# Weights loaded in the order of their first use, late ones prepared behind the first convolution, and x loaded already turned

## The reference

```python
xz = x @ W_in                                  # (16, 512, 128) @ (128, 512)
x_in, z = jnp.split(xz, 2, axis=-1)
xp = jnp.pad(x_in, ((0, 0), (3, 0), (0, 0)))
xc = conv_general_dilated(xp, dw_kernel[:, None, :], ...)   # 4 taps, depthwise
xc = silu(xc @ pw_kernel + conv_bias)          # then x_dbl = xc @ W_x, delta, the scan over 8 states,
...                                            # y * silu(z) @ W_out
```

## Time and profile before

| | |
|---|---|
| median of 3 runs | 2472.59 us (2466.28 to 2479.43) |
| the profiled execution | 2474.75 us, its span 2472.9 us |
| PE busy | 2107.4 us, 85% of the span |
| DVE busy | 1962.8 us, 79% |
| ACT busy | 1427.6 us, 58% |
| POOL busy | 808.0 us, 33% |
| mean granted TensorE clock | 0.951 |

### The profile page before, as it was taken

The page is one execution under the profiler, slowest core; times in us unless marked ns, Lnnn a source line. Parts: engine busy times, 40 slices in busy tenths (PEclk is TensorE's granted clock), DMA queues, the critical chain, the costliest instruction groups (busy, mean ns, idle before and its releaser), DMA issues. The chain is left out here.

```text
span 2472.9 us, 52605 instructions
## 1 busy us (share of the span) xinstructions
PE 2107.4 (85%) x15800; PEld 1560.8 (63%) x15929; DVE 1962.8 (79%) x3681; ACT 1427.6 (58%) x3256; POOL 808.0 (33%) x1060
## 2 busy tenths in 40 slices
PE   4389898989989898989898989899889849999980
PEld 1147565656657565657575656566566749999980
DVE  2787989798988888888988897989885447777768
ACT  2366766666667675666767666666655413333334
POOL 0111424141415141423324241414141333333337
PEclk9699999999999999999999999999989969999995
DMA  3452424152433324243424241524230042122117
GB/s 118 103 126 61 107 69 117 50 124 61 111 86 81 102 64 102 65 114 78 108 69 101 68 116 51 124 60 111 72 92 14 30 151 59 55 60 59 55 52 196
DMA packets 160526, 212.88 MB, mean 86 GB/s; under 512 B 20296, under 2 KB 97104, under 8 KB 160064
## 3 DMA queue, kind: packets, MB, share of 16 engines
q1 hardware_dynamic: 138192, 144.20, 19.7%
q0 software_dynamic: 22272, 67.92, 13.4%
HBM read 134.71 MB, written 28.08 MB: 66 GB/s over the span
## 5 line engine op out<-in xcount | busy, mean ns | idle before, releaser
L1432 DVE TENSOR_TENSOR_SCAN hs<-decay,push 128x512 f32<-128x512 f32 x256 | 320.1, 1272 | 7.1
L1184 ACT ACTIVATE S<-banks,fall_tok 128x128 f32<-128x128 f32 x1024 | 278.8, 385 | 27.7 <-PE banks L816 27.4
L1003 PE MATMUL banks<-rowsT,w_here 128*128 128x128 f32 x2176 | 269.6, 278 | 6.5 <-DVE w_here L1774 6.5
L1003 PEld LDWEIGHTS banks<-rowsT,w_here 128*128 128x128 f32 x2176 | 256.0, 193 | 10.1 <-issue 9.1
L1853 POOL DMA_DIRECT2D y<-ch x96 | 88.1, 918 | 477.2 <-DVE ch L1440 374.5
L1944 POOL TENSOR_TENSOR qd<-q,q_fall 128x512 f32<-128x512 f32 x96 | 159.4, 1660 | 208.7 <-ACT chunk_fall L1169 208.7
L1540 DVE TENSOR_TENSOR S<-banks,S 128x512 f32<-128x512 f32 x256 | 167.8, 683 | 64.2 <-PE banks L828 44.9
L1985 POOL DMA_INDIRECT results_scratch<-rows_out,result_to x136 | 132.2, 972 | 241.2 <-ACT rows_out L1310 234.5
L1425 DVE TENSOR_TENSOR push<-du,b_all 128x1024 f32<-128x1024 f32 x128 | 198.1, 1547 | 2.0 <-DMA b_all<-bc_scratch 2.0
L1299 ACT ACTIVATE tanh_h<-banks 128x512 f32<-128x512 f32 x136 | 81.3, 598 | 203.3 <-PE banks L1003 203.3
L1547 DVE SCALAR_TENSOR_TENSOR oT<-tog,banks 128x512 f32<-128x512 f32 x128 | 87.2, 681 | 136.0 <-ACT sq L1152 135.9
(11 more groups left out here) (221 smaller groups left out, 5096.5 us busy)
## 6 DMA issues: line engine op xcount, KB each, us to landing
y<-ch POOLq DMA_DIRECT2D x96, 512.0 KB, 5.5
b_all<-bc_scratch SPq DMA_DIRECT2D x128, 256.0 KB, 3.9
c_all<-bc_scratch SPq DMA_DIRECT2D x128, 256.0 KB, 3.6
q_fall<-fall_scratch SPq DMA_DIRECT2D x192, 128.0 KB, 3.3
rows_in<-rows_scratch SPq DMA_DIRECT2D x136, 66.0 KB
both<-results_scratch SPq DMA_DIRECT2D x32, 256.0 KB, 3.4
w<-w_dram SPq DMA_DIRECT2D x3, 2048.0 KB, 9.6
x_tok<-x_dram SPq DMA_DIRECT2D x16, 256.0 KB, 3.2
```

The source lines that it names most:

```text
L1003: mm = pe.matmul(bank_h[:, u % 2, n, here], w_here[:, u % 2, n, here], x, start=True, stop=True)
L1184: ins = nc.scalar.activation(S[:, g, here], bank[:, here], ACT.Exp, bias=fall_tok[:, head:head + 1])
L1432: nc.vector.tensor_tensor_scan(hs[:, h, :], decay[:, n % 2, h, :], push[:, h, :], 0.0, ALU.mult, ALU.add).then_inc(s_scan, 1)
```

## The change

- The loads are split in three, each on its own semaphore and in this order on SP: `conv_loads` (`w_inT`, `taps`, `pw`), then x of sequence 0, then `front_loads` (`b_conv`, `w_x`, `w_dt`, `b_dt`, `a_log`, `w_z`, `d_skip`), then the other 23.
- PE's fold waits for the first group alone; ACT waits for the second before it starts, since it begins with the exponential of `a_log`; PE waits for the second before the first sequence.
- `w_tap` has two places and the fold uses banks 0 and 1 in turn.
- DVE's preparation of `w_out`, `w_k`, `w_o`, `w_sign` and the token numbers goes into `prepare_late`, after its part of the first convolution in stage 2 of round 0. PE waits for it, and PE and ACT for the remaining loads, at the start of round 1, POOL for the loads before its first round.
- The host also gives x with features first (`xT`); SP loads it straight into the 512 columns of `xT`. `x_tok`, PE's four transposes, ACT's copy and the ring's use `xT` go away; 97 uses are left. The next load now waits until z of the sequence before has been multiplied (stage 6), in place of the turn (stage 0).

```diff
-FRONT = {"xT": 0, "u0": 1, "u1": 2, "xdbl": 3, "dt0": 4, "dt1": 4, "z0": 6, "z1": 6}
+FRONT = {"u0": 1, "u1": 2, "xdbl": 3, "dt0": 4, "dt1": 4, "z0": 6, "z1": 6}
...
-        w_tap = S[:, 1, 2 * P:4 * P].rearrange("p (c n) -> p c n", c=HALVES)
+        w_tap = S[:, 3, :].rearrange("p (s c n) -> p s c n", s=2, c=HALVES)
...
+        conv_loads = [(w_inT[:], a["w_inT"]), (taps[:], a["taps"]), (pw[:], a["pw"])]
+        front_loads = [
+            (b_conv[:], a["b_conv"]), (w_x[:], a["w_x"]), (w_dt[DT_ROW:DT_ROW + 8, :], a["w_dt"]), (b_dt[:], a["b_dt"]),
+            (a_log[:], a["a_log"]), (w_z[:], a["w_z"]), (d_skip[:], a["d_skip"]),
+        ]
...
-        PREPARED = 12 + PAIRS
+        PREPARED, PREPARED_LATE = 9, 3 + PAIRS
...
         @block.sync
         def _(sp):
+            for dst, src in conv_loads:
+                sp.dma_start(dst, src).then_inc(s_w_first, 16)
+            sp.dma_start(xT[:, TAPS - 1:TAPS - 1 + T], a["xT"][0]).then_inc(s_x_loaded, 16)
+            for dst, src in front_loads:
+                sp.dma_start(dst, src).then_inc(s_w_front, 16)
             for dst, src in loads:
                 sp.dma_start(dst, src).then_inc(s_weights, 16)
...
                     if not first(n):
-                        sp.wait_ge(ring.full_sem("xT"), ring.full_at("xT", n - 1))
-                    sp.dma_start(x_tok[:], x_dram[bass.ds(n, 1)].rearrange("b p c d -> (b p) c d")
-                                 ).then_inc(s_x_loaded, 16)
+                        sp.wait_ge(ring.full_sem("z1"), ring.full_at("z1", n - 1))
+                        sp.dma_start(xT[:, TAPS - 1:TAPS - 1 + T], a["xT"][bass.ds(n, 1)].rearrange("b d t -> (b d) t")
+                                     ).then_inc(s_x_loaded, 16)
...
         def _(pe):
-            pe.wait_ge(s_weights, WEIGHTS)
+            pe.wait_ge(s_w_first, 16 * len(conv_loads))
             for t in range(TAPS):
                 pe.wait_ge(s_wtap, HALVES * (t + 1))
-                if t >= 1:
-                    pe.wait_ge(s_wconv, t)
+                if t >= 2:
+                    pe.wait_ge(s_wconv, t - 1)
                 for c in range(HALVES):
-                    mm = pe.matmul(ring_banks[:, 0, 0:2 * P], w_tap[:, c, :], pw[:, c, :],
+                    mm = pe.matmul(ring_banks[:, t % 2, 0:2 * P], w_tap[:, t % 2, c, :], pw[:, c, :],
                                    start=(c == 0), stop=(c == 1))
                 mm.then_inc(s_wmul, 1)
             pe.wait_ge(s_wconv, TAPS)
             pe.wait_ge(s_prep, PREPARED)
+            pe.wait_ge(s_w_front, 16 * len(front_loads))
...
-            def turn_input(n):
+            def convolve(h, n):
                 pe.wait_ge(s_x_loaded, at(n, 16, 16))
-                turn("xT", x_tok, n)
-
-            def convolve(h, n):
-                bank, full = fill(ring, f"u{h}", n, "xT")
+                bank, full = fill(ring, f"u{h}", n)
...
             def body(i, j, n):
+                if i is not None and first(i):
+                    pe.wait_ge(s_weights, WEIGHTS)
+                    pe.wait_ge(s_prep_late, PREPARED_LATE)
...
         def _(act):
-            act.wait_ge(s_weights, WEIGHTS)
+            act.wait_ge(s_w_front, 16 * len(front_loads))
             nc.scalar.activation(a_neg[:], a_log[:], ACT.Exp).then_inc(s_alog, 1)
...
-            def turn_input(n):
-                nc.scalar.copy(xT[:, TAPS - 1:TAPS - 1 + T], full(ring, "xT", n)).then_inc(ring.free_sem("xT"), 1)
...
         def _(dve):
-            dve.wait_ge(s_weights, WEIGHTS)
+            dve.wait_ge(s_w_first, 16 * len(conv_loads))
             for t in range(TAPS):
-                if t >= 1:
-                    dve.wait_ge(s_wmul, t)
+                if t >= 2:
+                    dve.wait_ge(s_wmul, t - 1)
...
+            dve.wait_ge(s_w_front, 16 * len(front_loads))
+            nc.vector.tensor_scalar(b_conv[:], b_conv[:], 0.5, None, ALU.mult).then_inc(s_prep, 1)
             dve.wait_ge(s_alog, 1)
             nc.vector.tensor_scalar(a_neg[:], a_neg[:], -1.0, None, ALU.mult).then_inc(s_prep, 1)
             dve.wait_ge(s_prep, PREPARED)
+            def prepare_late():
+                dve.wait_ge(s_weights, WEIGHTS)
+                for w in (w_out, w_k):
+                    nc.vector.tensor_scalar(w[:], w[:], 0.5, None, ALU.mult).then_inc(s_prep_late, 1)
...
+                dve.wait_ge(s_prep_late, PREPARED_LATE)
...
+                    if h == FRONT["u1"] and first(n):
+                        prepare_late()
...
         def _(pool):
...
             pool.wait_ge(s_prep, PREPARED)
+            pool.wait_ge(s_weights, WEIGHTS)
```

More of the change, by code:

```diff
@@ L418, in build @@
         bank_y, bank_rows = banks[:, 4:6, :], banks[:, 6:8, :]
+        s_w_first = sem("conv_weights_loaded")
+        s_w_front = sem("front_weights_loaded")
         s_weights = sem("weights_loaded")
+        s_prep_late = sem("late_weights_prepared")
         s_wtap = sem("w_tap_ready")
@@ L1046, in _ @@
                 act.wait_ge(s_wmul, t + 1)
-                nc.scalar.activation(w_conv[:, t, :], ring_banks[:, 0, 0:2 * P], ACT.Copy, scale=0.5
+                nc.scalar.activation(w_conv[:, t, :], ring_banks[:, t % 2, 0:2 * P], ACT.Copy, scale=0.5
                                      ).then_inc(s_wconv, 1)
+            act.wait_ge(s_prep, PREPARED)
             def full(ring, use, it):
@@ L1256, in body @@
             def body(i, j, n):
+                if i is not None and first(i):
+                    act.wait_ge(s_weights, WEIGHTS)
                 if j is not None:
@@ L1356, in _ @@
             nc.vector.memset(state[:], 0.0).then_inc(s_prep, 1)
-            dve.wait_ge(s_weights, WEIGHTS)
+            dve.wait_ge(s_w_first, 16 * len(conv_loads))
             for t in range(TAPS):
-                if t >= 1:
-                    dve.wait_ge(s_wmul, t)
+                if t >= 2:
+                    dve.wait_ge(s_wmul, t - 1)
                 for c in range(HALVES):
-                    nc.vector.tensor_scalar(w_tap[:, c, :], w_inT[:, c, :], taps[:, c, t:t + 1], None,
+                    nc.vector.tensor_scalar(w_tap[:, t % 2, c, :], w_inT[:, c, :], taps[:, c, t:t + 1], None,
                                             ALU.mult).then_inc(s_wtap, 1)
-            for w in (b_conv, w_out, w_k):
-                nc.vector.tensor_scalar(w[:], w[:], 0.5, None, ALU.mult).then_inc(s_prep, 1)
-            for t in range(PAIRS):
-                nc.vector.tensor_scalar(w_o[:, t, :], w_o[:, t, :], norm_w[:, t:t + 1], 0.5 * HID ** 0.5, ALU.mult, ALU.mult
-                                        ).then_inc(s_prep, 1)
-            nc.vector.tensor_scalar(w_less, w_ffn[:], 0.0, None, ALU.is_lt).then_inc(s_sign, 1)
-            nc.vector.tensor_scalar(w_sign[:], w_ffn[:], 0.0, None, ALU.is_gt).then_inc(s_sign, 1)
-            dve.wait_ge(s_sign, 2)
-            nc.vector.tensor_tensor(w_sign[:], w_sign[:], w_less, ALU.subtract).then_inc(s_prep, 1)
-            nc.vector.tensor_scalar(x3_rows[:, :, TO], token_no[:], float(ALL_TOKENS - T), None, ALU.add
-                                    ).then_inc(s_token_no, 1)
-            dve.wait_ge(s_token_no, 1)
+            dve.wait_ge(s_w_front, 16 * len(front_loads))
+            nc.vector.tensor_scalar(b_conv[:], b_conv[:], 0.5, None, ALU.mult).then_inc(s_prep, 1)
             dve.wait_ge(s_alog, 1)
@@ L1410, in normalize @@
                                             ALU.subtract, ALU.mult).then_inc(done, 1)
-            def layer_norm(x, step, scale, done, it):
-                deviation(x, step, it)
-                normalize(x, scale, done, it)
             def state_part(n, part, i):
@@ L2058 @@
     arrays = {
-        "x": g["L0_attn_x"],
+        "x": g["L0_attn_x"], "xT": g["L0_attn_x"].transpose(0, 2, 1),
         "eye": c["eye"], "from_last": c["from_last"], "eye_bf": c["eye"].astype(bf),
```

28 lines of the change are left out of this document (15 added, 13 removed).

## The result

The changed kernel takes 2439.51 us (median of 4 runs, 2437.41 to 2441.41); the kernel before, measured with it, 2470.2 us (4 runs, 2466.28 to 2479.43). The ratio is 0.9873, 95% interval 0.9846 to 0.99. The forecast was 2449, so the direction is right, and the gain is 30.7 us in place of 23.7. ACT's copies of `x2T`, one for each sequence, divide that difference: 23.4 us of it are there at the first copy (129.54 before, 106.12 after), 9.3 come in the 15 rounds from the first copy to the last (1745.61 and 1736.29 us), and 0.6 behind them (597.75 and 597.13).

The account below looks back on a forecast made before the run. It took the start as unhidden and DVE, not PE, as ending stage 1 of steady rounds. 24.8 us gained at the start, 1.1 lost at round 2 and nothing in steady rounds gave 23.7 off 2472.59: 2449 us, range 2438 to 2459.

Parts of the forecast that it names:

- parts 1 to 3: Kernel start: split loads, two-place fold, preparation and turn out of the way; 24.8 us gained, bounds 19.5 and 26.5.
- part 2: Fold at the start: two places remove idleness, the clock rises after the second tap, taps three and four take 1.03 us each.
- rival (d): Fold at the start: the clock stays low, 2453 us, 3.8 more; a third of the forecast's chance, 0.65 with it included.
- Late weights: Round 0: late weights land near 22 us, preparation runs 22 to 25.5, hidden before DVE's task at 31; cost nothing.
- Turn to round 2: SP's new wait for z1 there delays b_all by 2.2 us; 1.1 us lost, the middle.
- the sum: Whole kernel: 24.8 us gained at the start less 1.1 lost at the turn to round 2, 23.7 us.
- the bound with 3.9 us to landing: Turn to round 2: b_all landing 3.9 us after issue would be there at 130.9, no loss.
- part 5: Steady rounds: PE's removed turn only lengthens its stage 1 wait for DVE; nothing gained, bounds 8.3 gained and 5 lost.
- Rounds stay at 116.4 us: Sign for the steady rounds: their length stays at 116.4 us after the change.
- wrong if rounds change by more than 0.3 us: Failure sign for the steady rounds: a change in their length above 0.3 us refutes the forecast.
- Rival (a): Steady rounds follow PE after all, so removing the turn gains 8 us more, 2441 us; chance 0.2.

## Why the prediction was right, and where not

- **Start (parts 1 to 3): the size right, a part of it by luck.** Weights at 4.33 (4.8 forecast), fold from 4.96 (5.4), second group at 7.54 (8.3), convolution at 12.08 (12.1), push of round 1 at 35.89 (about 35.6): 24.55 us against a sum of 24.8. The split of the loads and the early groups are as forecast.
- **The clock in the fold (part 2): this step was wrong, and two errors cancel.** I took two low taps of 2.07 us and two high ones of 1.03. But 2.05 is the time of a tap that stands alone, from its first start to its last end; the records of the old fold are 0.427 us apart as well, half of the 0.85 that the earlier trace rows show for 512 columns, so low taps in one stretch follow each 1.7 us. And the clock didn't rise after the second tap, near 8.4 us, but late in the fourth, near 10.9 (near 9.1 in the second execution). The fold took 6.65 us where 6.2 were forecast, and its earlier start makes up for it. Without any rise it would have ended near 12.1 and the convolution begun near 12.6, not at 14.2, by an estimate from the spacing of the records; so rival (d), with the 1.2 to 1.5 us of a convolution that starts low, was worth about 2 us and not 3.8.
- **Late weights: mis-sized, without effect.** I had them land near 22; they landed at 25.2, and the preparation ran from 25.17 to about 28.3 instead of 22 to 25.5. The cover has 3 us left before DVE's task at 31.39, not 5.5. The guess that they land as early as before, since the same bytes pass, did not hold.
- **Turn to round 2: mis-sized, and the sum fits by luck.** I took 1.1 us lost, the middle between 0 and 2.2; the runs put it at about 0.3, which can't be told from nothing, and DVE's wait for b_all, forecast to grow from 2.02 to about 3, was 1.77. The shift did shrink, from 24.55 us at the push of round 1 to 23.43 ahead of the turn, close to the 23.7 of the sum; but that was the low clock under the step sizes' product, not SP's wait. b_all is now issued 3.75 us ahead of the push that needs it (103.38 to 107.13), where it had been 6.08, so the bound with 3.9 us to landing was nearer than the middle.
- **Steady rounds (part 5): the mechanism right, the claim about their length wrong.** PE's wait in stage 1 grew from 1.39 to 1.93 (1.9 to 2.0 forecast), and with the clock granted in full a round is 115.04 before and 115.14 after. The load alone (0.9993) and the four transposes show it a second and third time. With x loaded only behind two pairs of b_all and c_all a round at full clock took 115.18, so SP's wait for z1 costs nothing there.
- **"Rounds stay at 116.4 us" and "wrong if rounds change by more than 0.3 us": this step failed.** 116.4 was the length of the one round I had read, one with a low stretch near 32 us, and I took it for the kernel's. The sum had no term for the clock in the rounds, although its price (0 to 3.4 us a round) is above every other of part 5, and the clock's row stands on the page. The granted clock of each round, and the runs in which only waits of PE were filled, showed it in its place. By that term the two executions of after come out at 2439.5 and 2451.0 us of span with the same code.
- **Rival (a)** named 2441, within 2 us of the result, and for the wrong reason. The turned load alone and the four transposes exclude it. A number that fits is no proof of its mechanism. The range reached down to 2438 only to take in this rival, so that it holds the measured 2439.5 is luck too.

What stays open: why the changed kernel met fewer low stretches in most executions. Four of its five runs lie at 2437 to 2441 us, and the new start alone gains 29.0 us as well, 5 to 6 more than the shift at its first copy (23.2 and 24.2 us against the two executions of the kernel before). So something of it seems to come with the new start; the load is not needed for it. But single executions of the variants that keep the new start took 2447 to 2450 us. That the rounds' state in one sets what the next finds is only argued, and no run separates it.

## What to carry over

Before a change in a loop is costed, list the length of every round and the granted clock beside it: one round read closely may be one of several kinds, and the kinds here differ by more than the edit did. Where PE waits a microsecond or so for another engine in each round, a few idle products in that wait can be worth more than useful work taken away. At a start, order the loads by their first use and give the first products two places to work in; it is the surest part of this change, 23 to 25 us each time. Time a product in a stretch by the spacing of its records, not by the length of one that stands alone.

## What the runs showed of the hardware that was not expected

- **A loop in which PE is busy 86% of the time can still lose TensorE's clock, and short waits have a part in it.** An opening with 1.01 and 0.68 us of waiting is followed by a granted clock of 0.72 over 6 us in some rounds and 1.00 in others; with both waits filled by 512-column bf16 products, none of 26 rounds in two kernels had a low opening. What decides between the two for the same waits stays open. The Trainium skill, page "TensorE: Matmul & The Clock Gate", section "A second HAM failure mode: psum-queue depth-cycling", tells of a kernel whose clock swings between the levels because PE idles briefly between groups of products. This trace agrees, with 1.02 and 1.92 us for the same products.
- **Less work for PE can start a low stretch.** Taking the turn out brought the stretches near 52 us (seven in rounds 2 to 14 of the first execution of after, none before), and four idle transposes in its place took them away again.
- **When the clock rises at a start varies between executions of one kernel.** In the same gapless fold it rose near 10.9 us in one and near 9.1 in the other, and the convolution began at 12.08 and 11.20.
- **A loop's jump back can cost several microseconds.** With 24 transposes more in PE's queue of a round, PE stood 5.8 us on issue in the mean at 12 of 12 jumps, where it else stands 1.01 us for DVE; with seven wide products, or the eight idle ones, there was none. The Trainium skill, page "Runtime: NRT & Kernel Launch", section "Instruction fetch mechanics", says that a taken branch to a target outside the engine's buffered instructions waits for them to be fetched. The runs fit that, since the kernel with the most records of PE in a round is the one that stands (1718 products and weight loads, against 1706 with the seven wide products); at which number it begins, they don't show.
- **A 512-column product of f32 with f32 weights takes 0.9 us** (6.28 us for seven, each two records), which made my filler twice as long as meant.
